# A four-layer graph network: GpSimd's scatter to the list by source waits for the last turned edge terms

## The chip, the cores and the metric

The kernel runs on one core of one Trainium2 chip. The metric is the device time of one execution in microseconds (us). A profiled execution gives the trace; its engines are called PE (TensorE's matrix multiplications), PEld (its weight loads), DVE (VectorE), ACT (ScalarE), POOL (GpSimd) and SP (SyncE, which only issues transfers here). "PEclk" is the share of full speed that TensorE's clock was granted.

## The reference, cut to what matters

Four graph layers run one after the other on 3125 nodes of 128 features and 100000 edges (`src`, `dst`, sorted by `dst`): a polynomial filter, an attention layer, a relational convolution with four edge types, and a second attention layer with edge features. Each adds its result to `x`.

```
h = relu(layernorm(x)); x = x + filter(h, src, dst)           # three sums over edges, by dst
h = relu(layernorm(x)); x = x + gat(h, edge_index)            # softmax over the edges of a dst
h = relu(layernorm(x)); x = x + relational(h, edge_type, edge_weight)   # three sums, by src
h = relu(layernorm(x)); x = x + attention(h, edge_attr_64 @ We + be, ...)
```

Two things are prepared ahead of the layers that this text is about. The filter layer needs, for each pair of nodes, how many edges join them (`counts`, 3200 x 3200), and the last attention layer needs `edge_attr_64 @ We + be` for each edge (the edge terms, 100000 x 8). The relational layer sums by `src`, though the edges come sorted by `dst`, so it needs a second list of the edges, sorted by `src`.

## The kernel before, in words

Edges lie one run of 784 (`EC`) to each of the 128 partitions. The program is a row of stages; `in_one_block` builds the streams of all five engines for one stage, and the next stage begins when all of them are through. Inside a stage the order of each engine is its program order, and semaphores alone tie the engines together. The stage of this text is `sort_and_count` (from L689). Its parts:

- **Places by source** (`places`, DVE, L256 to L309): where each edge goes in the list by source. Its last step raises `s_pos`.
- **Scatter to the list by source** (`send_edges`, L320 to L329, called by `gpsimd` at L751): 784 indirect transfers on GpSimd, one for each edge column. Each sends 128 records of 16 bytes, one from each partition, to 128 places of `by_src` in HBM (L326). They are written out one after the other, in groups of 7 over four semaphores; at most 28 transfers are out before GpSimd waits. The list is read again only in the relational layer (`read_list`, L1092).
- **Edge terms** (`attr_terms`, from L510): 14 groups of 7 chunks. For one chunk PE turns four 128x128 squares of edge features (L565), ACT copies them to SBUF (L600), and PE multiplies them with the weights (L579), eight terms for each edge. PE turns chunk c + 1 ahead of multiplying chunk c; ACT's copy of chunk c waits for PE's semaphore that chunk c is turned. After seven chunks ACT keeps the group (L647) and SP stores it (L665).
- **Turning the terms** (`turn`, `keep_turns`, `store_turns`, L603 to L641): when all groups are stored, SP reads them back (L632, L634), PE transposes them in 14 steps (L616), and ACT keeps each (L628) and raises `s_tkept`, which the caller knows as `attr["kept"]`, with `attr["groups"]` = 14.
- **The count loop** (`vector`, `tensor`, `scalar`, `sync`, L782 to L886): PE begins it only after `attr["kept"]` has reached 14, since it uses the same PSUM banks and the same SBUF space; DVE begins it when PE has summed the tile counts (L848, in PE's order behind the turning). For each of 25 windows of 128 `dst` nodes and each tile of 128 edges in it (806 visits in all), DVE makes `hot_src` (128 x 3200, 0 or 1, L757) and `hot_dst` (128 x 128, L759) and PE adds their product to seven PSUM banks (L824). DVE may be four visits ahead: it waits for `s_used`, which PE raises with the last matrix multiplication of a visit. Between two windows PE closes the banks (L869), ACT copies them out (L817), PE transposes them (L874), DVE copies them (L803), SP stores them (L884) and PE clears the banks (L862).

GpSimd has no work in this stage but the clearing at its start and the scatter. Edges are already sorted by `dst` in this input, so the sort ahead of the stage runs nothing.

Of the kernel before, what the change touches and what calls it, by code (L numbers as in the profile page):

```python
# [318 lines left out]
def send_edges(pool, s_out, rec, pos, table, base=0):  # L319


    for g in range(SENDS):
        if g >= R:
            pool.wait_ge(s_out[g % R], base + g // R * (16 * SEND))
        for e in range(g * SEND, (g + 1) * SEND):
            pool.indirect_dma_start(table, bass.IndirectOffsetOnAxis(ap=pos[:, e:e + 1], axis=0),  # L326
                                    rec[:, e, :], None).then_inc(s_out[g % R], 16)
    for r in range(R):
        pool.wait_ge(s_out[r], base + SENDS // R * (16 * SEND))  # L329
# [366 lines left out]
def sort_and_count(k, io, edges, tiles, unsorted):  # L696
# [6 lines left out]
    with ExitStack() as ctx:  # L703
# [34 lines left out]
        attr = attr_terms(k, io, ctx, unsorted, space)  # L738
# [3 lines left out]
        def gpsimd(pool):  # L742
            attr["gpsimd"](pool)
            pool.iota(idle[:, :], [[1, EC]], base=SLOTS, channel_multiplier=0,
                      allow_small_or_imprecise_dtypes=True).then_inc(s_io, 1)
            pool.iota(iota[:, :], [[1, NP]], base=-HALF, channel_multiplier=0,
                      allow_small_or_imprecise_dtypes=True).then_inc(s_io, 1)
            pool.iota(level[:, :], [[1, 1]], base=0, channel_multiplier=P,
                      allow_small_or_imprecise_dtypes=True).then_inc(s_io, 1)
            pool.wait_ge(s_pos, 1)  # L750
            send_edges(pool, s_sent, rec, pos, k.list_src)  # L751

# [125 lines left out]
        def sync(sp):  # L878
            attr["sync"](sp)
            sp.sem_inc(s_out, 16)  # L880
            with sp.Fori(0, W) as b:
# [3 lines left out]
                    .then_inc(s_out, 16)  # L885
            sp.wait_ge(s_out, 16 * W + 16)  # L886
        in_one_block(k, {"gpsimd": gpsimd, "vector": vector, "scalar": scalar, "tensor": tensor, "sync": sync})


# [1222 lines left out]
```

## Time and profile before

| | |
|---|---|
| median of 3 runs | 11653.21 us (11649.97 to 11662.95) |
| the profiled execution | 11657.24 us, its span 11655.4 us, 1.8 us around it |
| busy in the span | PE 47%, PEld 32%, DVE 34%, ACT 9%, POOL 47% |
| mean granted TensorE clock | 0.588 |
| `sort_and_count` | from 45.7 us to 2907.6 us of the span |

A line of the timeline reads: start in us, duration in us, engine, line of the kernel, operation, output<-inputs, shape, how many were merged, and in brackets how long the engine had been idle and what ended that ("issue" is nothing that the profile shows, "remote" is a semaphore event for which it finds no instruction). DMA-issuing instructions of GpSimd are shown with the time that GpSimd itself spends on them.

### The profile page before, as it was taken

To read this page: it belongs to the slowest core of one execution; us is meant where nothing else is said; L and a number is where in the kernel's file an instruction comes from. 1 tells how busy PE (TensorE), PEld (TensorE's weight loads), DVE (VectorE), ACT (ScalarE), POOL (GpSimd) and SP (SyncE) were. 2 spreads that over 40 slices of the span, in tenths; PEclk is the share of its full clock that TensorE was granted. 3 is DMA by queue.
4 is the path that set the end of the run, shared out by engine and by line. 5 is a ranking of instruction groups with operands and counts; after the bars stand their busy time and mean duration, and the time that the engine had idled before them with its cause. 6 is when DMAs were issued, how large, how long until landed. Compare 5 with 4: busy or idle time off the path is not lost. (4 is left out here: it accounts for less than half of the span.)

```text
span 11655.4 us, 136351 instructions
## 1 busy us (share of the span) xinstructions
PE 5446.2 (47%) x27089; PEld 3692.2 (32%) x27896; DVE 3972.8 (34%) x7942; ACT 1013.5 (9%) x3045; POOL 5474.2 (47%) x6919
## 2 busy tenths in 40 slices
PE   6000378887773333389533343333433323333433
PEld 5000244444332222279333333333333322222222
DVE  5000277666932111454311121111211133333444
ACT  1000000000001111122000000000000002222200
POOL 2777300000004666357366646666466635555445
PEclk6555699999885555555555555555555555555555
DMA  3000000011652333223211121112211121111100
GB/s 97 10 9 9 24 6 22 28 39 45 243 192 73 87 87 88 51 74 95 69 45 45 45 57 45 45 45 44 58 46 45 45 51 38 37 37 38 30 0 6
DMA packets 437253, 625.37 MB, mean 54 GB/s; under 512 B 107171, under 2 KB 320696, under 8 KB 425540
## 3 DMA queue, kind: packets, MB, share of 16 engines
q1 hardware_dynamic: 281534, 351.90, 9.5%
q0 software_dynamic: 155648, 272.65, 9.3%
q8 instruction: 30, 0.49, 0.0%
q14 instruction: 41, 0.34, 0.0%
HBM read 492.20 MB, written 131.99 MB: 54 GB/s over the span
## 5 line engine op out<-in xcount | busy, mean ns | idle before, releaser
L1151 POOL DMA_INDIRECT l_sum_rows<-l_table,l_sum_st x2448 | 2331.2, 952 | 1514.2 <-issue 785.0
L1250 PE MATMUL psum<-l_sum_rows,l_sum_hot 128*128 128x128 f32 x6528 | 1915.6, 458 | 2207.3 <-issue 1676.7
L1250 PEld LDWEIGHTS psum<-l_sum_rows,l_sum_hot 128*128 128x128 f32 x6528 | 1519.1, 322 | 2453.5 <-issue 2452.7
L1212 DVE TENSOR_SCALAR l_sum_hot<-iota,l_loc,l_weight 128x128 f32<-128x128 f32 x2448 | 666.0, 360 | 2875.4 <-remote 1900.3
L1411 POOL DMA_INDIRECT l_edges_by_src<-l_by_src,l_edges_st x816 | 809.7, 992 | 893.6 <-ACT l_edges_st L1437 438.8
L824 PE MATMUL psum<-hot_src,hot_dst 128*128 x4836 | 1100.5, 364 | 250.1 <-issue 217.0
L1411 POOL DMA_INDIRECT l_edges_by_src<-l_q,l_edges_st x816 | 788.1, 966 | 798.4 <-ACT l_edges_st L1450 411.6
L326 POOL DMA_INDIRECT by_src<-src_rec,src_pos x784 | 826.5, 1054 | 411.4 <-issue 244.5
L757 DVE TENSOR_SCALAR hot_src<-count_iota,tile_shifted 128x3200 f16 x806 | 850.7, 1056 | 293.5 <-PE psum L824 254.5
L974 POOL IOTA visit_number<- 128x816 f32 x1 | 0.8, 806 | 1830.1 <-POOLq L1345 1830.1
L824 PEld LDWEIGHTS psum<-hot_src,hot_dst 128*128 x5642 | 554.8, 99 | 793.7 <-issue 354.3
L1477 PE MATMUL psum<-l_k_parts,l_edges_hot_t 128*128 x2448 | 446.1, 290 | 648.0 <-issue 645.0
L579 PE MATMUL psum<-we_twice,attr_t 128*128 128x16 f32 x784 | 176.2, 366 | 983.1 <-issue 907.8
L1477 PE MATMUL psum<-l_dst_parts,l_edges_hot_t 128*128 x2448 | 381.5, 192 | 508.1 <-issue 475.5
L1477 PEld LDWEIGHTS psum<-l_k_parts,l_edges_hot_t 128*128 128x128 bf16 x2448 | 255.8, 104 | 853.3 <-issue 764.8
L1254 PE MATMUL psum<-l_sum_parts,l_sum_hot_bf 128*128 128x16 bf16 (+1 forms) x4896 | 403.0, 182 | 239.9 <-POOL l_sum_parts L1177 237.1
L1462 PE MATMUL psum<-ident_bf,l_edges_hot 128*128 128x128 bf16 x1640 | 240.0, 301 | 578.9 <-ACT l_edges_hot_t L1444 300.6
L1254 PEld LDWEIGHTS psum<-l_sum_parts,l_sum_hot_bf 128*128 128x128 bf16 x4896 | 397.8, 122 | 342.0 <-issue 257.3
L579 PEld LDWEIGHTS psum<-we_twice,attr_t 128*128 128x128 f32 x784 | 177.1, 331 | 1013.1 <-issue 934.8
L1704 PE MATMUL psum<-l_sum_counts,l_sum_rows 128*128 128x512 f32 (+1 forms) x1050 | 411.0, 555 | 155.8 <-DMA l_sum_counts<-counts 85.5
L1477 PEld LDWEIGHTS psum<-l_dst_parts,l_edges_hot_t 128*128 128x128 bf16 x2448 | 255.8, 104 | 668.8 <-issue 580.0
L1191 ACT COPY l_sum_st<-l_index 128x4 int32 x612 | 114.6, 194 | 3451.2 <-remote 2067.0
(346 smaller groups left out, 5602.4 us busy)
## 6 DMA issues: line engine op xcount, KB each, us to landing
l_sum_counts<-counts SPq DMA_DIRECT2D x75, 1600.0 KB, 7.6
l_rows<-l_edges_by_src SPq DMA_DIRECT2D x204, 256.0 KB
l_sum_rows<-l_rows SPq DMA_DIRECT2D x204, 256.0 KB, 2.6
counts<-attr_then_counts SPq DMA_DIRECT2D x25, 1600.0 KB, 7.1
l_sum_rows<-l_table,l_sum_st POOLq DMA_INDIRECT x2448
attr_then_counts<-in_edge_attr SPq DMA_DIRECT2D x14, 1568.0 KB
l_table<-l_rows SPq DMA_DIRECT2D x18, 1024.0 KB, 4.2
l_edges_by_src<-l_by_src,l_edges_st POOLq DMA_INDIRECT x816
```

The costliest lines, as they stand in the source:

```text
L326: pool.indirect_dma_start(table, bass.IndirectOffsetOnAxis(ap=pos[:, e:e + 1], axis=0), rec[:, e, :], None).then_inc(s_out[g % R], 16)
L579: ins = pe.matmul(k.ps[2 + g % 2][:, col:col + 2 * HEADS], attr_t[:, c % 2, a, :], we2[:, :, :].rearrange("p a b -> p (a b)"), start=False ...
L757: v.tensor_scalar(hot_src[:, bass.ds(place, 1), 0:NP].rearrange("p a c -> p (a c)"), iota[:, :], shifted[:, 0, bass.ds(t, 1)], None, ALU.i ...
L824: ins = pe.matmul(k.ps[c][:, 0:m], hot_dst[:, bass.ds(place, 1), :].rearrange("p a c -> p (a c)"), hot_src[:, bass.ds(place, 1), col:col + ...
L1151: pool.indirect_dma_start(rows[:, r, g, :], None, table, bass.IndirectOffsetOnAxis(ap=st[:, r, g:g + 1], axis=0))\
L1212: v.tensor_scalar(hot[:, r, g, :], k.iota[:, :], loc[:, n], weight[:, n], ALU.is_equal, ALU.mult).then_inc(s_hot[r], 1)
L1250: ins = pe.matmul(k.psum[:, bass.ds(to[g] * D, D)], hot[:, r, g, :], rows[:, r, g, :], start=False, stop=False)
L1254: ins = pe.matmul(k.psum[:, bass.ds(to[g] * n + 7 * PSUM_BANK, n)], hot16[:, r, g, :], parts[:, r, j, g, :], start=False, stop=False)
L1411: pool.indirect_dma_start(a[:, r, g, :], None, table_src, bass.IndirectOffsetOnAxis(ap=st[:, r, g:g + 1], axis=0))\
L1462: ins = pe.matmul(k.ps[q][:, g * P:(g + 1) * P], hot[:, q, g, :], k.ident16[:, :], start=True, stop=True)
L1477: ins = pe.matmul(by_place[:, q, g, 0:cols_dst], hot_t[:, q, g, :], by_dst[:, bass.ds(of[g], 1), j, :].rearrange("p a c -> p (a c)"), star ...
L1704: ins = pe.matmul(k.ps[b][:, 0:n], st[:, u, :], cnt[:, u, col:col + n], start=w == 0, stop=w == W - 1)
```

## The change

One wait is added on GpSimd, between its last iota and the wait for the places:

```diff
@@ gpsimd(pool) in sort_and_count
             pool.iota(level[:, :], [[1, 1]], base=0, channel_multiplier=P,
                       allow_small_or_imprecise_dtypes=True).then_inc(s_io, 1)
+            pool.wait_ge(attr["kept"], attr["groups"])
             pool.wait_ge(s_pos, 1)
             send_edges(pool, s_sent, rec, pos, k.list_src)
```

`attr["kept"]` is the semaphore that ACT raises with each of its 14 copies of turned terms (L628); PE waits for the same value before the count loop. Nothing is removed and no instruction but this one is added; all 784 scatters go from their place beside the edge terms to a place beside the count loop.

## Rows read from the trace of the kernel before

**Rows 1.** Stretches: us, then busy PE, PEld, DVE, ACT, POOL, clock, DMA share, GB/s.
```profile
223.60:1294.70 1071.10, 112.82 (x456) 92.24 (x454) 1.63 (x6) 22.93 (x41) 826.50 (x784) 0.50 0.06 10
1361.00:2908.00 1547.00, 1252.74 (x5811) 653.22 (x6617) 1070.57 (x1787) 81.71 (x200) 0.00 (x0) 0.96 0.09 25
```
**Rows 2.** Waits from 600 to 2600 us: total, times, longest.
```profile
ACT attr_t L600 <- remote: 732.0, 22, 38.2
DVE first_dst L787 <- PE psum L848: 1131.6, 1, 1131.6
```
**Rows 3.** Timeline: SP's stores of edge terms of the seventh and eighth group.
```profile
204.63 0.34 SPq L665 DMA_DIRECT2D attr_terms_by_edge<-attr_kept  x1
...
223.89 0.34 SPq L665 DMA_DIRECT2D attr_terms_by_edge<-attr_kept  x1
```
**Rows 4.** Timeline of ACT: chunk copies after the scatter's first transfer at 223.6 us.
```profile
232.29 0.58 ACT L600 COPY attr_t<-psum 128x512 f32<-128x512 f32 x1 [1.87 <-issue]
236.50 0.58 ACT L600 COPY attr_t<-psum 128x512 f32<-128x512 f32 x1 [3.62 <-remote]
246.40 0.58 ACT L600 COPY attr_t<-psum 128x512 f32<-128x512 f32 x1 [9.32 <-remote]
...
536.27 0.59 ACT L600 COPY attr_t<-psum 128x512 f32<-128x512 f32 x1 [33.01 <-remote]
```
**Rows 5.** Timeline of PE: one chunk's work while the scatter runs.
```profile
536.91 1.89 PE L579 MATMUL psum<-we_twice,attr_t 128*128 128x16 f32 x8 [30.78 <-issue]
538.64 1.09 PE L565 MATMUL psum<-ident,attr_then_counts 128*128 128x128 f32 x4
```
**Rows 6.** Timeline of POOL: the scatter where its pace changes.
```profile
489.89 0.97 POOL L326 DMA_INDIRECT by_src<-src_rec,src_pos  x1 [0.31 <-issue]
491.16 0.98 POOL L326 DMA_INDIRECT by_src<-src_rec,src_pos  x1 [0.30 <-issue]
...
493.84 1.10 POOL L326 DMA_INDIRECT by_src<-src_rec,src_pos  x1 [0.30 <-issue]
495.24 1.09 POOL L326 DMA_INDIRECT by_src<-src_rec,src_pos  x1 [0.30 <-issue]
```
**Rows 7.** Timeline from the scatter's last transfer to the count loop's first visit.
```profile
1293.69 0.97 POOL L326 DMA_INDIRECT by_src<-src_rec,src_pos  x1 [0.30 <-issue]
...
1321.68 1.07 ACT L600 COPY attr_t<-psum 128x512 f32<-128x512 f32 x2 [23.21 <-remote]
...
1331.41 0.32 SPq L665 DMA_DIRECT2D attr_terms_by_edge<-attr_kept  x1
...
1361.06 1.05 DVE L757 TENSOR_SCALAR hot_src<-count_iota,tile_shifted 128x3200 f16 x1 [2.21 <-issue]
```
**Rows 8.** Groups of the count loop: times, busy us, mean ns, idle before.
```profile
L757 DVE TENSOR_SCALAR hot_src<-count_iota,tile_shifted 128x3200 f16 x806 | 850.7, 1056 | 293.5 <-PE psum L824 254.5 <-issue 32.8
L824 PEld LDWEIGHTS psum<-hot_src,hot_dst 128*128 x5642 | 554.8, 99 | 793.7 <-issue 354.3
```
**Rows 9.** L757 alone from 1400 to 1600 us: DVE busy (times), clock, DMA share.
```profile
1400.00:1600.00 200.00, 127.25 (x121) 1.00 0.00 0
```
**Rows 10.** Timeline of DVE between the first two windows.
```profile
1622.71 1.06 DVE L757 TENSOR_SCALAR hot_src<-count_iota,tile_shifted 128x3200 f16 x1 [0.46 <-PE psum L824]
...
1635.78 1.05 DVE L757 TENSOR_SCALAR hot_src<-count_iota,tile_shifted 128x3200 f16 x1 [0.61 <-issue]
```
**Rows 11.** Timeline of POOL, and of DVE, in a gather stage of the attention layer.
```profile
4319.07 0.94 POOL L1411 DMA_INDIRECT l_edges_by_src<-l_by_src,l_edges_st  x1 [0.30 <-issue]
4320.32 1.36 POOL L1411 DMA_INDIRECT l_edges_by_src<-l_by_src,l_edges_st  x1 [0.31 <-ACT l_edges_st L1450]
...
4320.18 0.69 DVE L1421 TENSOR_TENSOR l_edges_hot<-loc,iota 128x512 bf16<-128x512 f32 x1 [0.47 <-issue]
```
**Rows 12.** PE's register instructions, without and with gathers beside them: min/median/max ns.
```profile
L824 PEldq FUSED_REGOPS  x5642: 46/46/132, 1362.9 to 2900.4; - x195
...
L1250 PEldq FUSED_REGOPS  x3264: 2/135/1408, 5013.9 to 9435.6; - x192
```

## The prediction, written before the changed kernel was run

> **What bounds the kernel now.** No single engine does, so the place of the change is read by stretches. While the scatter runs, from 223.6 to 1294.7 us, PE is busy 113 of 1071 us, DVE 2, ACT 23, and GpSimd alone works [rows 1]. The count loop that follows takes 1547 us with no GpSimd work at all [rows 1]. The two stretches lie one behind the other though nothing in the data asks for it; what joins them is seen in the waits: DVE sits 1131.6 us until PE, behind the edge terms in its own order, sums the tile counts [rows 2]. So the edge terms set the start of the count loop.
>
> And they are slow only beside the scatter. Before it a group of seven chunks takes 223.89 - 204.63 = 19.26 us [rows 3], a chunk 0.58 + 1.87 = 2.45 us [rows 4]. After its first transfers ACT's copies come 4.21 and 9.90 us apart, and later 33.60 us, with 33.01 us of idling that ends with "remote" [rows 4]; 22 such waits make 732 us [rows 2]. PE's own instructions keep their length: 1.89 us for the eight matrix multiplications of L579, 1.09 us for the four of L565 [rows 5]. They are done at 539.73 us and ACT, which needs only them, starts at 536.27 + 33.60 = 569.87. What is late is PE's semaphore. With as many weight loads, a chunk has 24 PE instructions, and 33.60 / 24 = 1.40 us.
>
> The same 1.40 us is the scatter's. Its transfers begin 1.27 us apart up to 491 us and 1.40 us apart from then on [rows 6]. I read this as something behind GpSimd that takes 1.40 us for each: 0.13 us of surplus per transfer, 210 transfers by 491 us, 27 us piled up; and when the scatter is over, the last late copy comes 1321.68 - 1294.66 = 27 us later [rows 7]. The two agree, so I take it that PE's semaphores suffer by the size of that pile: nothing up to 232.29 us (7 transfers, 0.9 us), 1.76 us late at 236.50 (10 transfers, 1.3 us), and worse from there. It is an inference from paces; no row names the resource.
>
> **The change, step by step.** *The wait itself* holds GpSimd until ACT's fourteenth kept turn. Behind it on GpSimd is only the scatter; nobody waits for the scatter inside the stage except the stage's end, and the list is read thousands of us later. All 784 transfers move; SP's stores of the counts (25 of them) are the only transfers that they now meet.
>
> *Edge terms without the scatter.* At 223.89 us eight stores are out [rows 3]. Each store comes after the second chunk of the next group, so the thirteenth is at 223.89 + 5 x 19.26 = 320.2; the last has no two chunks of a next group ahead of it and comes 19.26 - 2 x 2.45 = 14.4 us later, at 334.6. From the last store to the first visit the trace has 1361.06 - 1331.41 = 29.65 us [rows 7], which stays: the terms are read back, turned and kept. First visit at 364.2: **997 us earlier**. The scatter starts some 4 us ahead of it.
>
> *The scatter beside the count loop.* A visit takes 200 / 121 = 1.65 us [rows 9], 1.06 us of it L757 [rows 8]. Does the pile grow? In the attention layer a gather that meets a DVE operation of 0.69 us takes 1.36 us of GpSimd instead of 0.94 [rows 11], 0.42 more. No row has L757 beside a transfer. Bounds for what it adds to each: 0, and 1.06 us, the whole operation. If a transfer waits out the L757 that it meets, the pace is one for each visit, 1.65 us; that is more than 1.40, the pile empties and PE is not disturbed. An addition of 0.13 us is already enough. I take 0.38 us (1.65 - 1.27), near the 0.42 of [rows 11].
>
> The Trainium skill ("SBUF — State Buffer", section Who interferes with whom) says that a DVE operation in a two-port mode blocks GpSimd fully until it ends, as would hold for L757. It is there too that PE and ACT never wait on anyone. By that second rule the chunks would have stayed at 2.45 us beside the scatter, the change would bring nothing; 33.60 us in [rows 4] speaks against it.
>
> *Between windows* DVE makes no `hot_src` for 12.0 us [rows 10]: 9 transfers at 1.27 us, a pile of 1.2 us, just under the 1.3 us of the first late copy. I charge each of the some 17 changes inside the scatter one such lateness, 1.76 us: +30 us. Lower bound 0; the upper is rival 1.
>
> *The visits.* DVE has 1.65 - 1.30 = 0.35 us of slack in each, so a short collision is hidden. PE's register instructions, 46 ns here and at most 132, reach 1408 ns where gathers run [rows 12]; seven weight loads [rows 8] stand in a visit. I take nothing, and as the other bound 0.35 us for each of 784 visits, +275 us.
>
> *Scatter's end*: 784 x 1.65 = 1294 us at most, before the loop's 1547 are over: hidden. Sum against the profiled execution: 11657.24 - 997 + 30 = 10,690 us (it lies 4 us above the median of the runs, 11653.21). This case's own range is 10,660 to 10,950.
>
> **Rival 1: the pile comes back inside the loop.** If at one change of windows it passes the point where PE's semaphores are late, DVE starves, nothing slows GpSimd, and the state holds until the scatter ends. At the first change (364 + 1622.71 - 1361.06 = 626 us [rows 7, 10]): 614 transfers are left, 614 x 1.366 (1071 / 784) + 27 = 866 us. In these PE does the change, 7 closings, 25 transposes and 7 clearings with their weight loads, 78 instructions at 1.40 = 109 us, then one visit in 19.6 us (14 instructions) to 30.8 (with eight more on registers): 25 to 39 visits, 41 to 64 us of normal work. The rest of the loop, about 1220 us, follows: 2712 against 2908, so 11,461. Later changes give less loss, down to 10,900. For it: the thin margin, 1.2 against 1.3. Against it: four visits in a row after each change.
>
> **Rival 2, slower: caught from the first visit.** The scatter has 4 us ahead of DVE, and DVE's first four visits come 1.3 us apart, which slows it little. If the pile passes the point there, the loop crawls through the whole scatter: 364 to 360 + 1071 + 27 = 1458 us, 1094 us in which 36 to 56 visits are done (59 to 92 us of work). Against the old start at 1361 that is 97 us late, less 59 to 92: +5 to +38 us, **11,662 to 11,695**. It decides at 97 / 1.65 = 59 visits done: below that the change loses. For it: beside the scatter every PE semaphore in the trace became late within 13 us. Against it: DVE had then nothing to do.
>
> **Rival 3: the scatter starves.** If a transfer gets through only in every second visit (3.30 us), the loop's 1547 us take 381 in visits and 227 between windows, 176 are left, 224 us at 1.27 behind the loop: 364 + 1547 + 224 = 2135 against 2908, 10,884 us. The Trainium skill ("SBUF — State Buffer", section Summary: rules for kernel authors) advises against hiding a GpSimd-issued transfer under DVE operations in the fast modes for this reason.
>
> **How the numbers follow.** A measurement of this kernel tells about 0.2%, 23 us, from no change. Forecast 0.43, rival 1 0.20, rival 3 0.05, rival 2 0.32, wide since it hangs on a pile of 1 us. The first three are faster: 0.68. Rival 2 is split by its own span at +23 us: 0.12 same, 0.20 slower, the half with register instructions counted being likelier. The range has to take in rival 2 to hold 0.8: 10,655 to 11,700; it is bimodal, with little between 11,500 and 11,650.
>
> **What would show each step.** L600's copies stay 2.45 us apart to the last group and SP's last L665 is at about 335 us; first L757 near 364; POOL L326 one for each L757, its duration 1.3 us or so, over by 1650; L757 still x121 in 200 us; first copies of L817 near 632. Wrong: L757 coming 20 to 30 us apart with idling ended by "remote" or PE, L326 still at 1.27 to 1.40 us, and the clock of the loop's first 1000 us near 0.5 rather than 0.96; then rival 1 or 2, told apart by where it begins. If L326 reaches past the loop, rival 3.

## The result: 1.8% faster, by the way of rival 1, and the profile after

The kernel after takes 11,445.1 us (median of 4 runs, 11,441.58 to 11,457.03) against 11,655.22 us before: ratio 0.9825, 95% interval 0.9813 to 0.9837. I had forecast 10,690 us. The gain is 210 us, not 965. The time lies 16 us from rival 1's 11,461, and 4 us from it by the profiled executions for which that sum was made (11,657.24 before, 11,457.03 after).

The same kernel before has a median of 11,599 to 11,655 us in some measurements and of 9,511 to 9,523 us in others, with no median between and the runs of one measurement within 0.3% of each other, but for a single one of 14,368 us at a granted clock of 0.398; I call the first the **long** and the second the **short** condition. The traces of before and after are both of the long one.

The page of the kernel after, DVE's busy share and the clock in 40 slices of 286 us:

```profile
DVE  5520056667821111544311121112211133333444
...
PEclk6865589998875555555555555555555555555555
```

DVE has work in the second slice, hardly any in the third (2 tenths), none to speak of in the next two, and then goes on: the count loop started, nearly stood still and recovered. The stretches say when (columns as in [rows 1]):

```profile
360.00:640.00 280.00, 221.21 (x1015) 114.69 (x1174) 196.35 (x325) 4.86 (x12) 226.51 (x166) 0.98 0.03 5
640.00:1000.00 360.00, 52.61 (x115) 16.39 (x133) 27.09 (x43) 0.00 (x0) 275.80 (x275) 0.53 0.04 6
...
1470.00:2710.00 1240.00, 981.08 (x4553) 512.16 (x5157) 820.66 (x1376) 78.43 (x192) 8.38 (x8) 0.94 0.11 31
```

The edge terms ran as forecast. Timeline of ACT, the last group and the last turned terms, and of DVE, the first visit (L758 is before's L757; all lines behind the new one are one higher):

```profile
333.53 0.59 ACT L600 COPY attr_t<-psum 128x512 f32<-128x512 f32 x1 [1.87 <-PE psum L565]
336.76 0.53 ACT L647 COPY attr_kept<-psum 128x448 f32<-128x448 f32 x1 [2.64 <-PE psum L579]
...
362.53 0.33 ACT L628 COPY attr_turned<-psum 128x64 f32<-128x64 f32 x2 [0.82 <-DMA attr_terms<-attr_turned]
366.96 1.05 DVE L758 TENSOR_SCALAR hot_src<-count_iota,tile_shifted 128x3200 f16 x1 [2.21 <-issue]
```

So the loop starts 1361.06 - 366.96 = 994 us earlier [rows 7]. For one window it runs as it did alone. Then comes the first change of windows. Timeline of DVE from the last visit ahead of it to the first ones behind it:

```profile
628.58 1.06 DVE L758 TENSOR_SCALAR hot_src<-count_iota,tile_shifted 128x3200 f16 x1 [0.44 <-PE psum L825]
...
645.22 0.69 DVE L804 COPY attr_then_counts<-psum 128x512 f32<-128x512 f32 x1 [15.42 <-remote]
652.92 0.69 DVE L804 COPY attr_then_counts<-psum 128x512 f32<-128x512 f32 x1 [7.01 <-remote]
...
702.80 1.05 DVE L758 TENSOR_SCALAR hot_src<-count_iota,tile_shifted 128x3200 f16 x1 [1.99 <-issue]
...
1502.30 1.06 DVE L758 TENSOR_SCALAR hot_src<-count_iota,tile_shifted 128x3200 f16 x1 [16.98 <-remote]
1507.30 1.05 DVE L758 TENSOR_SCALAR hot_src<-count_iota,tile_shifted 128x3200 f16 x1 [3.78 <-PE psum L825]
```

A change that took 13.1 us before [rows 10] takes 74.2; then a visit comes every 18 to 20 us, until 27.6 us after the scatter's last transfer, which starts at 1479.67. It isn't PE's semaphores alone that are late, as the prediction had it. DVE's second operation of a visit (L760) follows the first (L758) after 0.97 us while all is well, and here after 2.80 = 2 x 1.40 us, and PE's matrix multiplications themselves start 1.40 us apart with nothing to wait for that the profile shows:

```profile
709.54 1.06 DVE L758 TENSOR_SCALAR hot_src<-count_iota,tile_shifted 128x3200 f16 x1 [5.52 <-issue]
712.34 0.26 DVE L760 TENSOR_SCALAR hot_dst<-count_iota,tile_shifted  x1 [1.74 <-issue]
...
752.94 0.58 PE L825 MATMUL psum<-hot_src,hot_dst 128*128 x1 [0.81 <-issue]
754.34 0.58 PE L825 MATMUL psum<-hot_src,hot_dst 128*128 x1 [0.81 <-issue]
```

GpSimd at the first change:

```profile
628.40 1.36 POOL L326 DMA_INDIRECT by_src<-src_rec,src_pos  x1 [0.30 <-issue]
630.06 0.97 POOL L326 DMA_INDIRECT by_src<-src_rec,src_pos  x1 [0.30 <-issue]
631.34 0.97 POOL L326 DMA_INDIRECT by_src<-src_rec,src_pos  x1 [0.30 <-issue]
```

Beside DVE's visits a transfer takes 1.36 us and they come 1.65 us apart; as soon as DVE rests they take 0.97 and come 1.27 us apart. L758 alone, in three stretches (DVE's busy time and times; clock, DMA share):

```profile
366.00:630.00 264.00, 168.99 (x160) 0.98 0.02 1
630.00:1503.00 873.00, 50.88 (x44) 0.53 0.03 3
1503.00:2697.00 1194.00, 635.43 (x603) 0.95 0.11 32
```

In 873 us 44 visits are made, which with one change of windows are worth 44 x 1.65 + 13 = 86 us. So 787 us of the 994 are given back here; the last visit is at 2695.31 instead of 2895.43 us, 200 us earlier, which is the gain of the profiled execution (11,657.24 to 11,457.03).

### The profile page after: what moved, and what is told of

Its sections match the earlier page's. It is cut to its first block and busy times, and to the rows that moved or that the text cites. A ratio compares the mean times of both kernels' runs of the same rounds, so it can differ in the third digit from the quotient of the medians.

```text
span 11455.2 us, 136352 instructions
## 1 busy us (share of the span) xinstructions
PE 5487.4 (48%) x27089; PEld 3697.4 (32%) x27896; DVE 3977.1 (35%) x7942; ACT 1014.4 (9%) x3045; POOL 5519.0 (48%) x6919
## 5 line engine op out<-in xcount | busy, mean ns | idle before, releaser
L825 PE MATMUL psum<-hot_src,hot_dst 128*128 x4836 | 1155.7, 376 | 928.4 <-DVE hot_src L758 541.2
L758 DVE TENSOR_SCALAR hot_src<-count_iota,tile_shifted 128x3200 f16 x806 | 855.3, 1061 | 1016.4 <-remote 699.7
L326 POOL DMA_INDIRECT by_src<-src_rec,src_pos x784 | 873.0, 1114 | 550.4 <-ACT attr_turned L628 306.0
L1822 DVE COPY l_own<-psum 128x36 f32 x204 | 39.4, 193 | 1039.1 <-remote 575.5
L1934 DVE TENSOR_TENSOR l_edges_by_src<-l_edges_by_src,psum 128x512 f32<-128x512 f32 x204 | 139.7, 685 | 743.6 <-remote 695.7
```

What stands on the lines that cost most here:

```text
L758: v.tensor_scalar(hot_src[:, bass.ds(place, 1), 0:NP].rearrange("p a c -> p (a c)"), iota[:, :], shifted[:, 0, bass.ds(t, 1)], None, ALU.i ...
L825: ins = pe.matmul(k.ps[c][:, 0:m], hot_dst[:, bass.ds(place, 1), :].rearrange("p a c -> p (a c)"), hot_src[:, bass.ds(place, 1), col:col + ...
L1934: v.tensor_tensor(a, a, b[:, :, 0:D], ALU.mult).then_inc(s_p, 1)
```

## The experiments

Theory A is the prediction's: a pile behind GpSimd, drained at 1.40 us for each transfer, and no lateness where there is no pile. Theory B: GpSimd's transfers make PE's semaphores late at any pace. Theory C: the change of windows does it by itself. Which condition a measurement finds can't be chosen: e1 to e8, e11 to e15 and e17 fell into the short one, e9, e10, e16 and e18 into the long one. e15 and e18 ran on one and the same chip, so the condition is no fixed property of a chip.

### Slower transfers, and transfers tied to visits (e1 to e4, short condition)

e1 and e2 change the kernel before, e3 the kernel after (memset of 128x128, of 128x1 in e2); e4 ties the transfers to PE's visits:

```diff
@@ e1 to e3, send_edges: behind each transfer
+                pool.wait_ge(idled, e)
+                pool.memset(idle, 0.0).then_inc(idled, 1)
@@ e4, send_edges: ahead of transfer e
+                pool.wait_ge(used, e + 4)
```

> The kernel before, with a GpSimd memset of 128x128 behind each of the 784 transfers of the scatter, so that they start further apart (1.27 us without it; the memset should add some 0.2 us, pace about 1.45). Theory A (pile: something behind GpSimd takes 1.40 us for a transfer, and PE's semaphores are late by the size of what has piled up): at a pace over 1.40 us nothing piles up, the edge terms' chunks stay 2.45 us apart beside the scatter, the count loop starts near 364 us as in the kernel after, with the scatter running on beside it; about 10,660 to 10,720 us, 930 to 1000 below the kernel before, by added work on GpSimd alone. Theory B (transfers of GpSimd beside PE's work make PE's semaphores late at any pace): chunks still some 30 us apart, 11,650 us or more (the scatter lasts 784 x 1.45 = 1137 us instead of 1071: up to 11,720).

> As e1, with a memset of 128x1, the shortest one (some 0.1 us): pace about 1.37 us, just under 1.40. Theory A: the pile still grows, by 0.03 us a transfer, so the first late copy comes after some 40 transfers and not 10, and from then on it is as before: 11,600 to 11,660 us. If the memset costs over 0.13 us the pace passes 1.40 and the time is that of e1. Theory B: 11,650 to 11,700, the first copy late at once.

> The kernel after, with the memset of 128x128 behind each transfer. Theory A: at the change of windows GpSimd's pace is then about 1.45 us instead of 1.27, nothing piles up, no visit is late; the stage is that of the forecast: 10,660 to 10,720 us. Theory B: the first change of windows (or even the first visit, since each transfer now also meets a memset) is late as in the kernel after: 11,400 us or more. Theory C (the change of windows itself is what hurts: SP's store of counts or ACT's copies meeting the scatter's queue): 11,400 us or more as well, with the copies of L804 late at 645 us.

> The kernel after, with each transfer waiting until PE has done as many visits (transfer e waits for visit e - 1), so that GpSimd pauses at each change of windows and can't run ahead when PE is late. Theory A: pace 1.65 us inside a window, none between windows, no pile: 10,655 to 10,700 us, scatter through with visit 784 near 1900 us. Theory B: PE late all the same, 11,000 us or more.

Measured: 9514.2, 9511.5, 9513.1 and 9512.8 us against 9511.5 us for the kernel before beside them; all four ratios lie between 1.0000 and 1.0002, intervals of 0.1% around. No theory had foreseen that: the kernel before itself was 2,140 us shorter. The four tell nothing of A against B, only that there was nothing to cure. They gave the price of the pause: pace = 0.97 + memset + 0.17 us, so 1.26 us with 128x1 and 1.36 with 128x128.

### The two kernels unchanged in the short condition (e5, e6), and the same cures again (e7, e8)

> The kernel before, unchanged, with a profile of its own. e1 to e4 ran on another chip than the traces of before and after, where the kernel before takes 9511 us, not 11,653; no trace shows how its scatter runs there. Theory A: on such a chip what lies behind GpSimd takes at most 1.27 us for a transfer, so there is no pile anywhere: copies of L600 2.45 us apart beside the scatter (1.27 us apart, never 1.40), first L757 near 366 us. On a chip like the first one: copies of L600 up to 33.6 us apart, the scatter 1.40 us apart from about 490 us, 11,650 us. Theory B (the chips differ in something that has nothing to do with GpSimd's transfers, such as PE's semaphores being slow by themselves): PE's semaphores late with no transfer about, too.

> The kernel after, unchanged, beside e5 on the same chip. On a chip without the pile theory A gives no difference, 9511 us within 0.2%: the edge terms take as long with and without the scatter, and in the count loop the scatter is hidden in both. On a chip like the first one: 11,445 us, 0.9825 of before. Theory B gives the same two numbers.

> The kernel before with a memset of 128x320 behind each transfer. In e1 and e2 the pace was 0.97 us + the memset + 0.17 us (1.36 us with 0.22, 1.26 with 0.12), so this one should be about 1.50 us. On a chip like the first one: theory A 10,660 to 10,720 us, copies of L600 2.45 us apart, since 1.50 us is over 1.40; theory B 11,650 us or more, up to 11,750 since the scatter lasts 784 x 1.50 us. On a chip where before takes 9511 us: no change in either.

> The kernel of e4 (after, each transfer waiting for a visit of PE) again. On a chip like the first one: theory A 10,655 to 10,700 us, no visit late; theory B 11,000 us or more. On a chip where before takes 9511 us: no change.

Measured: e6, the change as it is, 9519.1 against 9518.8 us, ratio 1.0000 (0.9990 to 1.0009); e7 1.0007 (0.9997 to 1.0017); e8 0.9999 (0.9989 to 1.0008). So the change is worth nothing here. The timeline of e5 (the kernel before, unchanged) shows why: ACT beside the scatter, DVE at the first change of windows:

```profile
253.62 0.59 ACT L600 COPY attr_t<-psum 128x512 f32<-128x512 f32 x1 [1.87 <-PE psum L565]
256.08 0.59 ACT L600 COPY attr_t<-psum 128x512 f32<-128x512 f32 x1 [1.87 <-PE psum L565]
...
631.93 1.06 DVE L757 TENSOR_SCALAR hot_src<-count_iota,tile_shifted 128x3200 f16 x1 [0.45 <-PE psum L824]
...
640.52 3.88 DVE L803 COPY attr_then_counts<-psum 128x512 f32<-128x512 f32 x7 [7.38 <-PE psum L874]
```

and the stretch beside the edge terms (columns as in [rows 1]):

```profile
226.00:360.00 134.00, 119.33 (x539) 109.38 (x538) 1.31 (x6) 29.68 (x53) 102.00 (x106) 0.51 0.39 103
```

The copies that came 33.60 us apart [rows 4] come 2.45 apart, beside a scatter at 134 / 106 = 1.26 us; the loop starts at 370.2 us in the kernel before too, and a change takes 13.1 us with the scatter beside it. No wait in the whole trace ends with "remote", where the long condition has seven groups of them, 6,487 us of waiting. Theory B as "always" is out: in this condition PE doesn't mind transfers at 1.27 us.

### Is 1.40 us a time for each transfer, and whose? (e9, e10, long condition)

e9 puts 784 transfers of 32 records ahead of the full ones; e10 adds SP's small transfers to the kernel after:

```diff
@@ e9, gpsimd of the kernel before
+            send_edges(pool, s_sent, rec, pos, k.list_src, rows=32)
-            send_edges(pool, s_sent, rec, pos, k.list_src)
+            send_edges(pool, s_sent, rec, pos, k.list_src, SENDS // R * (16 * SEND))
@@ e10, sync of the kernel after, at the start of each window
+                for j in range(64):
+                    sp.dma_start(k.small[bass.ds(b * 64 + j, 1), :, :].rearrange("a p e -> p (a e)"),
+                                 iota[:, 0:8]).then_inc(s_small[j % 4], 16)
```

> The kernel before, with 784 additional transfers of 32 records each (a quarter) ahead of the 784 full ones, so that GpSimd starts them faster than one in 1.27 us; what they write is written again by the full ones. e5 showed no pile at 1.27 us on this chip. Theory A (a fixed time for each transfer behind GpSimd, here below 1.27 us): if the pace falls under that time, copies of L600 come late as in the kernel before on the first chip, up to 24 times the pace apart; the pace at which the scatter then settles is that time. Theory A2 (time by the number of records): a quarter takes a quarter, nothing piles up, copies stay 2.45 us apart. Time in both: the stage is a little over that of e5, about 9520 us, in A later by as much as the edge terms are late.

> The kernel after, with 64 additional transfers of 128 x 16 bytes by SP at the start of each window of the count loop (1600 in all, SP issues one in some 0.34 us), beside the scatter. Theory A, if the place behind GpSimd is one that SP's transfers share: a pile at each start of a window, visits (L758) late there and after, the scatter's pace at other than one for each visit; 9,600 us or more. If it is GpSimd's own: visits 1.65 us apart, 9,515 us. Theory B: no change either.

Measured in e9: 12,601.3 against 11,598.7 us, ratio 1.0863 (1.0831 to 1.0895), not the 9,520 that I wrote for the short condition. POOL's timeline, a little before the pace changes and where it does, and ACT's copies ahead of that:

```profile
371.56 0.87 POOL L326 DMA_INDIRECT by_src<-src_rec,src_pos  x1 [0.30 <-issue]
372.74 1.08 POOL L326 DMA_INDIRECT by_src<-src_rec,src_pos  x1 [0.30 <-issue]
374.12 1.09 POOL L326 DMA_INDIRECT by_src<-src_rec,src_pos  x1 [0.31 <-issue]
...
259.84 0.59 ACT L600 COPY attr_t<-psum 128x512 f32<-128x512 f32 x1 [23.91 <-remote]
293.44 0.59 ACT L600 COPY attr_t<-psum 128x512 f32<-128x512 f32 x1 [33.01 <-remote]
```

A transfer of a quarter of the records still costs GpSimd 0.87 us; they come 1.17 us apart and then, from the 126th, 1.40 us apart, as the full ones do. So the 1.40 us is for a transfer, not for its records. And the pile can be measured: the number of transfers ahead of the first one that takes GpSimd longer, times 1.40 us, less the time from the first of them to that one. Stretch of e9 with its transfers (POOL's busy time, times):

```profile
224.00:372.80 148.80, 109.07 (x126) 0.50 0.09 21
```

The first starts at 224.78 and the 126th, the first longer one, at 372.74: 125 x 1.40 - 147.96 = 27.0 us. The kernel before: 211 transfers from 223.63 to 492.44 us, 26.6 us. The kernel after: 264 from 630.06 to 973.68 us, 26.0 us. At three surpluses (0.23, 0.13 and 0.13 less collisions) the pile is full at 26 to 27 us, which is 19 transfers. With the 27 us that everything needs to recover after the last transfer [rows 7] and the 27.6 us of the kernel after, that is the strongest evidence for a queue of fixed length behind GpSimd; what it is in the chip no row names. It isn't the program's own limit of 28 transfers: in the kernel before all 783 idle times of GpSimd between these transfers end with "issue", 0.31 us on average, and it is the transfer itself that grows, from 0.97 to 1.09 us [rows 6].

Measured in e10: 11,423.1 against 11,598.7 us, ratio 0.9847 (0.9819 to 0.9876), as the kernel after does without the additional transfers. SP issued them 0.56 us apart in the first window (I had said 0.34), 64 in 36 us, and no visit was late (columns as in [rows 1]; then the next stretch, where the fall comes at the change all the same):

```profile
360.00:640.00 280.00, 254.94 (x1177) 115.27 (x1177) 196.64 (x325) 4.98 (x13) 226.47 (x165) 0.98 0.05 7
640.00:1000.00 360.00, 61.67 (x138) 17.07 (x138) 28.54 (x45) 0.00 (x0) 276.03 (x276) 0.52 0.06 7
```

What piles up is GpSimd's own; SP's transfers don't feed it. But SP suffers from it: later in the scatter its small transfers come 54.6 / 13 = 4.2 us apart, and each has three instructions of SP (L885 has a MOVE, the transfer and a FUSED_REGOPS), so that is 1.40 us for each of them, too:

```profile
901.86 54.61 SPq L885 DMA_DIRECT2D small<-count_iota  x14
```

### The cures once more (e11 to e14, short condition again)

The kernels of e7, e1 and e4, and the kernel after with the memset of 128x320:

> The kernel of e7 (before, memset of 128x320 behind each transfer, which in e7 set them some 1.5 us apart) for a chip like that of the traces of before and after, where the kernel before takes some 11,600 us (as e9 and e10 had it). Theory A (something behind GpSimd takes 1.40 us for a transfer, and PE's semaphores are late by the size of the pile): no pile at 1.5 us, copies of L600 2.45 us apart, first visit near 366 us, 930 to 1000 us under before. Theory B (GpSimd's transfers make PE's semaphores late at any pace, one transfer for one PE instruction): copies 24 x 1.5 = 36 us apart, same time as before or up to 70 us more.

> The kernel of e1 (before, memset of 128x128: 1.36 us apart) on such a chip: just under 1.40. Theory A: the pile still grows, by 0.04 us for a transfer, so the first late copy comes after some 30 transfers, not 10; then as before: within 60 us of before. Theory B: within 60 us of before, first late copy at once.

> The kernel of e4 (after, each transfer waits for a visit of PE) on such a chip. Theory A: GpSimd stops at each change of windows and whenever PE is late, no pile: visits 1.65 us apart throughout, 950 to 1000 us under before. Theory B: visits late as in the kernel after, each transfer then as late as they: 200 us under before at best.

> The kernel after with the memset of 128x320 behind each transfer, on such a chip. Theory A: over 1.40 us at the changes of windows, too, no pile: 930 to 1000 us under before, without any pause of GpSimd. Theory C (the change of windows itself, by its store or its copies, is what hurts): as the kernel after, 210 us under before.

Measured: 1.0008 (0.9998 to 1.0017), 1.0001, 0.9997, and for e14 9624.3 against 9514.0 us, 1.0115 (1.0099 to 1.0132). Nothing on the theories. e14 is a miss of its own: beside DVE's `hot_src` a transfer and its memset come some 2.2 us apart, the memset at a mean of 0.67 us, so 784 of them reach past the loop; POOL's last one starts at 2000.0 us, when the last visit has been made at 1910.9:

```profile
L326 POOL DMA_INDIRECT by_src<-src_rec,src_pos x784: 974/1148/1802, 364.8 to 2000.0; - x196
```

A pace is safe only where the scatter starts early or is short.

### Five paces in one kernel (e15 short, e16 long condition)

Since the condition comes by chance, one kernel was made to hold all the cases. Transfer by transfer, in the kernel before:

```diff
@@ send_edges: (first transfer, memset columns or "visit", visit to wait for)
+ plan=[(0, 320, 0), (90, 'visit', 0), (220, 320, 130), (300, 128, 240), (400, 0, 350), (500, 'visit', 460)]
```

> The kernel before, its 784 transfers in six stretches, so that one trace shows several paces: transfers 0 to 89 with a memset of 128x320 behind each (some 1.5 us apart, beside the edge terms); 90 to 219 each waiting for one more visit (visits 0 to 130); 220 to 299 with the memset of 128x320 and no wait (from visit 130); 300 to 399 with a memset of 128x128 (1.36 us apart where DVE rests; from visit 240); 400 to 499 bare, 1.27 us apart where DVE rests (from visit 350); 500 to 783 each waiting for one more visit again (from visit 460). On a chip like that of e9 and e10 (before 11,599 us there): theory A: copies of L600 2.45 us apart at 1.5 us; visits undisturbed in the three stretches that follow, over their changes of windows (at 1.36 us a change lets 9 transfers through, a pile of -0.4 us); in the bare stretch visits late from its first change of windows on (9 x 0.13 = 1.2 us of pile); and undisturbed again soon after the wait for visit 460 has let the pile drain. Total some 11,599 - 997 + 100 = 10,700 us. Theory B (any pace): copies 36 us apart from the start, the same time as before or more. Theory C (the change of windows itself): visits late from the first change in the third stretch on. On a chip where before takes 9514 us: no change, nothing late anywhere.

> The kernel of e15 once more, for a chip like that of e9 and e10 (e15 fell on one where before takes 9519 us). Theory A there: copies of L600 2.45 us apart beside transfers 1.5 us apart; visits undisturbed in the stretches tied to visits, with the long memset and with the short one; late from the first change of windows of the bare stretch (transfers 400 to 499), undisturbed again after the pause for visit 460; some 10,700 us against 11,600. Theory B: copies 36 us apart from the start, 11,600 us or more. Theory C: visits late from the first change of windows in the stretch with the long memset on.

Measured: e15 0.9998 (0.9987 to 1.0009). e16, **10,773.5 against 11,603.2 us, ratio 0.9282** (0.9255 to 0.9309). Theory A gave 10,700, B 11,600 or more. Its trace, one stretch after the other. POOL beside the edge terms, 1.52 us apart, and ACT there:

```profile
300.67 0.98 POOL L335 DMA_INDIRECT by_src<-src_rec,src_pos  x1 [0.17 <-issue]
301.64 0.39 POOL L339 MEMSET slow<- 128x320 f32 x1
302.19 0.98 POOL L335 DMA_INDIRECT by_src<-src_rec,src_pos  x1 [0.17 <-issue]
...
299.61 0.59 ACT L613 COPY attr_t<-psum 128x512 f32<-128x512 f32 x1 [1.87 <-PE psum L578]
302.06 0.59 ACT L613 COPY attr_t<-psum 128x512 f32<-128x512 f32 x1 [1.87 <-PE psum L578]
```

In the long condition, beside 90 transfers, not one chunk is late, where 10 transfers at 1.27 us were enough in [rows 4]. Theory B is out there too. The changes of windows, from DVE's last visit on (with the long memset; with the short one; bare; tied to visits):

```profile
749.71 1.06 DVE L773 TENSOR_SCALAR hot_src<-count_iota,tile_shifted 128x3200 f16 x1 [0.47 <-PE psum L840]
...
758.28 3.88 DVE L819 COPY attr_then_counts<-psum 128x512 f32<-128x512 f32 x7 [7.17 <-issue]
...
844.79 1.23 DVE L773 TENSOR_SCALAR hot_src<-count_iota,tile_shifted 128x3200 f16 x1 [0.47 <-PE psum L840]
...
853.93 0.69 DVE L819 COPY attr_then_counts<-psum 128x512 f32<-128x512 f32 x1 [7.76 <-PE psum L890]
858.15 0.69 DVE L819 COPY attr_then_counts<-psum 128x512 f32<-128x512 f32 x1 [3.52 <-remote]
...
1014.50 1.05 DVE L773 TENSOR_SCALAR hot_src<-count_iota,tile_shifted 128x3200 f16 x1 [0.45 <-PE psum L840]
...
1030.31 0.69 DVE L819 COPY attr_then_counts<-psum 128x512 f32<-128x512 f32 x1 [14.59 <-remote]
...
1367.42 1.05 DVE L773 TENSOR_SCALAR hot_src<-count_iota,tile_shifted 128x3200 f16 x1 [0.41 <-PE psum L840]
...
1379.05 3.88 DVE L819 COPY attr_then_counts<-psum 128x512 f32<-128x512 f32 x7 [10.41 <-PE psum L890]
```

| at the change | pace of GpSimd, us | last visit to first copy, us | last visit to next, us |
|---|---|---|---|
| e5, short condition | 1.27 | 8.6 | 13.1 |
| long memset | 1.52 | 8.6 | 13.1 |
| short memset, first change | 1.36 | 9.1 | 27.7 |
| short memset, second change (6 transfers, then a stop) | 1.36 | 10.4 | 14.2 |
| tied to visits (7 transfers, then a stop) | 1.27 | 11.6 | 15.4 |
| bare | 1.27 | 15.8 | 69.8 |
| kernel after | 1.27 | 16.6 | 74.2 |

Theory C is out: a change with GpSimd at work is undisturbed at 1.52 us. The bare stretch fell at its first change, as the kernel after did. Then GpSimd pauses from transfer 500 on:

```profile
1148.06 1.06 DVE L773 TENSOR_SCALAR hot_src<-count_iota,tile_shifted 128x3200 f16 x1 [5.87 <-remote]
```

The last bare transfer starts at 1136.89 us and everything is well from 1148.06 on, 11 us later and not 27: the pile of 94 transfers in 122.2 us is 94 x 1.40 - 122.2 = 9.4 us. The recovery goes with the pile, which B can't explain. In the third stretch my working had a wrong sign: at 1.36 us nine transfers leave a pile of +0.4 us, not -0.4. A has a pile there, but one far under the 1.3 us that the prediction took for the point, so I had expected nothing, and its first change took 27.7. It recovered with no stop of GpSimd.

### The whole cure, and the gather loops (e17 short, e18 long condition)

The kernel before with plan=[(0, 320, 0), (90, 'visit', 0)], and behind each gather of `edge_rows` (L1411) a memset:

```diff
@@ edge_rows, gpsimd
+                        pool.wait_ge(s_idle, i * (R * G) + r * G + g + 1)
+                        pool.nop(nofuse=True)
+                        pool.memset(idle[:, :], 0.0).then_inc(s_idle, 1)
```

> What e16 showed, made into a version: the kernel before, transfers 0 to 89 of the scatter with a memset of 128x320 behind each (1.5 us apart, beside the edge terms), all others waiting for one more visit each; and the same cure where it has not been tried, in the two gather loops of the attention layers (816 gathers each): a memset of 128x256 and a wait for it behind each gather, some 1.47 us from one to the next. On a chip that shows the effect: theory A: last visit near 1960 us (e16: 2057, of which some 100 are its bare stretch and its short memset), and the two gather loops, 1263 and 1432 us long before, take 816 x 1.47 = 1200 us each, since PE's semaphores then come in time: 11,600 - 950 - 60 - 230 = 10,360 us. If in the gather loops something else than the pile holds PE back, they stay as long as they were or get longer, 10,600 to 10,750 us. On a chip that doesn't: the scatter costs nothing, the two gather loops get 816 x 0.2 = 160 us longer each, 9,840 us.

> The kernel of e17 once more, for a chip that shows the effect (on e17's, where before takes 9523 us, it costs 349 us, in the two gather loops). Theory A there: last visit near 1960 us and the two gather loops 1200 us each instead of 1263 and 1432: 10,360 us against 11,600. If the gather loops are held by something else: 10,600 to 10,750 us.

Measured: e17 9872.0 us, ratio 1.0369 (1.0349 to 1.0390). e18 **10,583.5 against 11,643.9 us, ratio 0.9089** (0.9071 to 0.9107), better than the change; but I had expected 10,360, and it lies just under the range (10,600 to 10,750) that I had given for gather loops held by something else. Its stage holds: last visit at 1943.7 us (expected 1960), 952 us earlier than in the kernel before. The two gather loops (columns as in [rows 1]; first the kernel before, then e18):

```profile
3565.00:4828.00 1263.00, 494.21 (x3242) 328.10 (x3242) 196.98 (x604) 153.23 (x405) 808.27 (x815) 0.50 0.33 87
9581.00:11013.00 1432.00, 559.89 (x3238) 323.90 (x3237) 526.48 (x1208) 325.76 (x1213) 786.96 (x815) 0.50 0.13 37
```

```profile
2610.00:3876.00 1266.00, 482.53 (x3252) 327.70 (x3252) 202.59 (x609) 153.93 (x406) 1055.73 (x1630) 0.50 0.36 87
8629.00:9947.00 1318.00, 551.43 (x3234) 322.05 (x3232) 524.31 (x1203) 323.87 (x1211) 1052.87 (x1630) 0.50 0.16 40
```

The first isn't shorter at all, the second by 114 us of the 232 expected; with the 952 us of the stage that is the whole gain. DVE still waits 753.5 us for "remote" in the first (632.3 before) and 311.3 in the second (702.2 before). At 1.44 us from gather to gather the engines are still late there, so for these gathers a pace over 1.40 us is no cure. Whether a gather of 512 bytes a row takes more than 1.40 us behind GpSimd, or the other traffic of that loop counts, stays open.

## Why the prediction failed, step by step

*The pile* was right, and for the scatter it is now shown rather than inferred: the pace of 1.40 us is reached with the same 26 to 27 us behind GpSimd from two different paces, it holds for a quarter of the records, recovery takes as long as the pile is, and a pace above it removes the effect (e9, e16). *What it does to PE* was half wrong. The prediction has PE's semaphores "suffer by the size of that pile"; but in the kernel before the chunk copy of this row is already 33.60 us behind the one ahead of it, when some 7 us are piled up (56 x 0.13), as with 27 us in [rows 4]:

```profile
295.48 0.59 ACT L600 COPY attr_t<-psum 128x512 f32<-128x512 f32 x1 [33.01 <-remote]
```

How large the pile is decides how long the recovery takes. The lateness is one PE instruction for each 1.40 us whatever the size, and it can meet DVE and SP as well (the rows of L760 and of e10). That was in the prediction's own division 33.60 / 24 and in rival 1, not in its forecast.

*Edge terms without the scatter*: last copy of a group at 336.76 us where I had the last store at 334.6; first visit 366.96 instead of 364.2, so 994 us instead of 997. Right.

*The scatter beside the count loop*: 1.65 us apart, one for each visit, 1.36 us each: 0.39 more than the 0.97 at rest, against the 0.38 taken. Inside the first window L758 lost nothing (160 visits in 264 us, 160 in 263 before). Right. The Trainium skill ("SBUF — State Buffer", Who interferes with whom) has GpSimd blocked while such a DVE operation runs; these rows agree: the transfer that starts at 628.40 us ends at 629.76, 0.12 us behind the L758 that it meets (628.58 to 629.64), and L758 isn't lengthened. Its other rule there, that PE never waits on anyone, fits the short condition and not the long one, though no row shows whether SBUF's ports, which that rule is about, have a part in it.

*Between windows* is **the step that failed**: "9 transfers at 1.27 us, a pile of 1.2 us, just under the 1.3 us of the first late copy. I charge each of the some 17 changes inside the scatter one such lateness, 1.76 us". The 1.3 us came from the edge terms, where one copy waits for one semaphore. At a change PE has 78 instructions to bring through, and each late one lengthens the change, in which GpSimd goes on at 1.27 us. So the term that was charged 1.76 us for each change, +30 us in all, measured 74.2 - 13.1 = 61 us at the first one, and then the loop didn't recover: some 787 us in all. The runs put the point much lower: with the short memset, where nine transfers leave a pile of 9 x 0.04 = 0.4 us, the second of the copies comes 4.2 us behind the first (undisturbed, all seven fit in 3.88), and in the kernel after the first copy is 8 us late, with 12 transfers out. What decides isn't one size of the pile but whether GpSimd stops or slows down: with 7 transfers and a stop a change costs 15.4 - 13.1 = 2.3 us, close to my 1.76; at 1.36 us with no stop it costs 14.6 and recovers; at 1.27 us with no stop it doesn't recover before the transfers end or pause. I saw the margin of 0.1 us, and gave rival 1 0.20 where it deserved the first place: an edge read off one row, with a feedback behind it.

*Rival 1's sum* held: 866 us of late semaphores were worked out, 630.06 to 1507.30 is 877; 25 to 39 visits in it, 44 made; 109 us for the change, 74.2 measured, and the shorter change and the visits at the short end of 19.6 to 30.8 us left room for the additional ones; 11,461 against 11,457 in the profiled execution.

*Rivals 2 and 3* didn't come: the first four visits were 1.13 us apart (the prediction had 1.3) and nothing was late behind them, and no transfer took GpSimd more than 2.44 us.

*Scatter's end*: at 1480 us, hidden in the loop. Right, but the sum had some 1650: most transfers ran at 1.27 to 1.40 us beside a loop that stood nearly still, not at 1.65.

What the prediction didn't hold at all is the condition: in the short one the change is worth 1.0000 (e6).

## What to carry to other kernels

Where an engine starts transfers faster than they are taken (here 1.27 against 1.40 us), no edge can be read off one row: ask what the engine that is made late does to the one that starts them, and if the answer is "nothing", count on the whole fall. Tie it to the other's progress, or give it a pause: 90 memsets and waits on a semaphore that was there already end the stage 952 us earlier in the long condition (e18) and cost nothing in the short one (last visit at 1903 us in e17, 1905 in e5). And measure such a change in more than one place: it is worth 1.8% here or nothing, by a condition that the program doesn't show.

## What the runs showed of the hardware that was not expected

- The same kernel takes 9,511 to 9,523 us or 11,599 to 11,655 us; one chip showed both (9,519 beside e15, 11,644 beside e18). The difference lies beside GpSimd's indirect transfers: with one after the other 1.25 us apart the five gather loops of 816 take 1,018 to 1,040 us each in the short condition (e5), 1,186 to 1,432 in the long one (the kernel before), 1,147 us together, and the count loop's last visit comes 991 us later; that is all of the 2,121 us between the two traces, within 1%. What sets the condition no run shows.
- In the long condition GpSimd can be 26 to 27 us ahead of what takes its transfers, at 1.40 us for each, whether it carries 128 records or 32. While enough waits there, PE's instructions come through one for each transfer (24 in 33.6 us, [rows 4]; matrix multiplications that start 1.40 us apart in the kernel after). DVE's and SP's can be late in the same steps (2.80 and 4.2 us for two and three instructions), though SP's transfers don't add to the pile (e10).
- A transfer of 32 records costs GpSimd 0.87 us, one of 128 records 0.97: nearly all of it is the same for both.
